# Scores of a local attention by query halves as 64x64 tiles of TensorE, a block-diagonal product as 128x32 tiles, and some reordering in the first half

## What is computed

```python
h = layernorm(x) * (1 + ca) + sa
x = x + ga * attn(h)        # 3 layers: causal linear attention, 16 heads, FFN of 1024
h = layernorm(x) * (1 + cb) + sb
x = x + gb * ffn(h)         # 2 layers: local attention, 8 heads of 64, gated FFN of 682
...
def causal_linear_attention(q, k, v):      # first half, per token
    S += k v^T ; z += k
    out = (q S) / (q z + 1e-6)
...
def local_attention(q, k, v):              # second half, windows of 128 tokens
    # queries of window w see keys of windows w-1 and w
    mask = (i < j) | (i > j + 128) | (j == -1)
    attn = softmax(where(mask, -max, (8 q) k^T))
    out = attn v
```

## Time and profile before

| | |
|---|---|
| median of 3 runs | 2609.28 us (2607.87 to 2610.86) |
| the profiled execution, its own time | 2610.22 us |
| its span | 2608.4 us |
| PE busy | 2523.3 us, 97% |
| DVE busy | 2143.9 us, 82% |
| ACT busy | 1405.0 us, 54% |
| POOL busy | 1427.1 us, 55% |
| mean granted TensorE clock | 0.989 of full |

### The profile page before, as it was taken

How to read it: one execution, slowest core, us unless ns; L and a number is a source line. 1 busy time by engine, 2 the same in 40 slices (tenths; PEclk the granted TensorE clock), 3 DMA queues, 4 the chain that set the end, 5 groups by cost and what they waited for, 6 DMA issues and landing times.

```text
span 2608.4 us, 65564 instructions
## 1 busy us (share of the span) xinstructions
PE 2523.3 (97%) x23520; PEld 2094.4 (80%) x23520; DVE 2143.9 (82%) x5253; ACT 1405.0 (54%) x2945; POOL 1427.1 (55%) x1406
## 2 busy tenths in 40 slices
PE   6899999999999999999998999999999999999998
PEld 4688888888888888887776788888888888888877
DVE  5798888887787788898999887888898887888875
ACT  3343344334433443344256777777776777777761
POOL 2253444443444355455576666666676766776664
PEclk8899999999999999999999999999999999999999
DMA  3100000010000010000112000000111100110001
GB/s 91 38 18 10 18 2 18 14 36 2 2 2 14 14 42 10 18 26 26 49 38 66 21 17 19 12 16 17 32 32 36 33 29 23 32 32 28 27 29 49
DMA packets 79088, 67.44 MB, mean 26 GB/s; under 512 B 15896, under 2 KB 73368, under 8 KB 78776
## 3 DMA queue, kind: packets, MB, share of 16 engines
q1 hardware_dynamic: 78776, 63.25, 8.1%
HBM read 49.18 MB, written 12.58 MB: 24 GB/s over the span
## 4 chain that ended last, share of the span: by engine, by line
PE 87%; DVE 6%; issue 3%; ACT 2%; POOL 1%; DMA 0%; SPq 0%; DVEq 0%; ACTq 0%; POOLq 0%
PE PS L276 76%; PE PS L974 4%; PE PS L936 1%; PE PS L1004 1%; PE PS L927 1%; PE PS L488 1%; PE PS L498 1%; PE PS L431 1%; PE PS L885 1%; DVE U L3159 1%; DVE PS L3567 1%; PE PS L1034 1%; DVE Z L2997 0%; ACT PR L2227 0%; DVE X L3005 0%
## 5 line engine op out<-in xcount | busy, mean ns | idle before, releaser
L2227 ACT ACTIVATE PR<-PS,SM 128x256 f32<-128x256 f32 (+1 forms) x512 | 280.7, 561 | 136.5 <-DVE SM L3572 135.9
L1913 ACT ACTIVATE FB<-PS,BC 128x512 f32<-128x512 f32 x192 | 133.5, 695 | 322.1 <-PE PS L276 174.9
L3159 DVE TENSOR_TENSOR U<-PS,CST 128x512 f32<-128x512 f32 x384 | 238.0, 681 | 37.5 <-PE PS L276 37.4
L4597 POOL TENSOR_TENSOR RL<-FB,RH 128x512 fp32r<-128x512 f32 x96 | 125.7, 1310 | 219.6 <-DVE RH L3136 219.6
L4819 POOL TENSOR_TENSOR SM<-SM,COL 128x8 f32<-128x8 f32 x128 | 224.6, 1755 | 10.7
L276 PE MATMUL PS<-W2H,RH 128*128 128x256 f32 x768 | 226.1, 294 | 2.2 <-POOL RL L4597 2.2
L3567 DVE CUSTOM_DVE_ANT_0 PS<-PS,MSK 128x256 f32<-128x256 f32 (+1 forms) x512 | 202.5, 436 | 30.5 <-PE PS L276 29.5
L276 PE MATMUL PS<-W2H,RL 128*128 128x256 f32 x768 | 215.8, 281 | 0.0
L276 PE MATMUL PS<-W2L,RH 128*128 128x256 f32 x768 | 215.7, 281 | 0.0
L4609 POOL TENSOR_TENSOR SBD<-SBD,TMP 128x256 f32<-128x256 f32 x84 | 64.8, 772 | 197.0 <-DVE TMP L3151 197.0
L276 PEld LDWEIGHTS PS<-W2H,RH 128*128 128x128 f32 x768 | 145.0, 189 | 25.0 <-issue 20.4
(11 more groups left out here) (268 smaller groups left out, 8467.4 us busy)
## 6 DMA issues: line engine op xcount, KB each, us to landing
PX<-in_L_attn_x SPq DMA_DIRECT2D x16, 512.0 KB, 3.9
TB<-in_k_rot SPq DMA_DIRECT2D x64, 128.0 KB, 2.1
SG<-in_L_attn_W SPq DMA_DIRECT2D x24, 256.0 KB, 2.8
xp_scratch<-PX SPq DMA_DIRECT2D x8, 512.0 KB, 2.9
xs_scratch<-X SPq DMA_DIRECT2D x64, 64.0 KB, 1.5
ZS<-xs_scratch SPq DMA_DIRECT2D x16, 256.0 KB, 2.8
GG<-xp_scratch SPq DMA_DIRECT2D x7, 512.0 KB, 3.7
out<-GG SPq DMA_DIRECT2D x7, 512.0 KB, 2.9
```

Of the source, the lines that this page charges most:

```text
L1913: e.activation(FB[:, hb % 2, :], PS[:, 5, :], ACT.Relu, bias=BC[:, l % 2, 4 + hb:5 + hb]).then_inc(*a_re.up(n, hb))
L2227: t = e.activation(PR[:, par, 256 * i + lo:256 * i + hi], PS[:, 3 + par, 256 * i + lo:256 * i + hi], ACT.Exp, bias=S[:, 40 + 2 * g + i:41 ...
L3159: e.tensor_tensor(heads(U[:, u % 6, :], 4), heads(PS[:, g, :], 4), bcast(CM, 4), ALU.mult).then_inc(*d_mk.up(n, u))
L4597: e.tensor_tensor(RL[:, r, :], FB[:, 0, :], RH[:, r, :].bitcast(F), ALU.subtract).then_inc(*p_rl.up(n, hb))
```

## The change

1. `scores_tile` splits the 128 queries in two halves of 64. A matmul now has 64 rows and 64 columns (par picks the rows, half the columns and the output partitions), and multiplies 192 keys instead of 256: for the lower half the whole window before and the lower 64 keys of its own, for the upper half the upper 64 keys of the window before and its whole own window. The region left out is the one that the mask covers.
2. The keys are stored with the two buffers beside each other for each pair of heads (`keys_of`), so that for odd tiles the 192 keys are one run of columns, and one matmul. For even tiles the window before lies behind the own window, and each half has two matmuls, of 128 and 64 keys or 64 and 128. Columns of scores, PR and PT now always have the window before first, so `blocks`, the masks and the copies lose their cases.
3. In `sums` the product with SBD is made of four matmuls of 32 columns instead of one of 128.
4. DVE: for chunks 1, 2 and 23 both `add_bv` steps stand ahead of `gate_steps(1)` and `modulate_b(2)`, of `modulate_a(3)`, and of `norm2_b(20)`.
5. PE, end of the first half: `up(22, 1)` stands ahead of `down(21, 6)` and `up(22, 5)` ahead of `ask_v(0)`.

```diff
+    def keys_of(b):
+        return KT.rearrange("p x (h b n) -> p (x h) b n", h=2, b=2)[:, :, b, :]
...
                 for m in range(2):
-                    mm(e, PS[:, 4, 128 * m:128 * m + 128], SBD[:, tile % 2, m, :], FQ[:, m, 0, 128 * j:128 * j + 128], m == 0)
+                    for g in range(4):
+                        mm(e, PS[32 * g:32 * g + 32, 4, 128 * m:128 * m + 128], SBD[:, tile % 2, m, 32 * g:32 * g + 32], FQ[:, m, 0, 128 * j:128 * j + 128], m == 0)
...
             for i in range(2):
+                c = 128 * (2 * hf + i)
                 for par in range(2):
-                    r, c = slice(64 * par, 64 * par + 64), slice(128 * (2 * hf + i), 128 * (2 * hf + i) + 128)
-                    if first:
-                        m = mm(e, PS[:, 3 + par, 256 * i + 128 * cur:256 * i + 128 * cur + 128], QT[r, c], KT[r, cur, c], i == 0)
-                    else:
-                        m = mm(e, PS[:, 3 + par, 256 * i:256 * i + 256].rearrange("p (b n) -> p b n", b=2), QT[r, c], KT[r, :, c], i == 0)
+                    for half in range(2):
+                        r, p, a = slice(64 * par, 64 * par + 64), slice(64 * half, 64 * half + 64), 256 * i
+                        Q = QT[r, c + 64 * half:c + 64 * half + 64]
+                        if first or cur == 0:
+                            before, here = 128 if half == 0 else 64, 64 if half == 0 else 128
+                            if not first:
+                                mm(e, PS[p, 3 + par, a + 128 - before:a + 128], Q, keys_of(1 - cur)[r, 2 * hf + i, 128 - before:128], i == 0)
+                            m = mm(e, PS[p, 3 + par, a + 128:a + 128 + here], Q, keys_of(cur)[r, 2 * hf + i, 0:here], i == 0 and first)
+                        else:
+                            m = mm(e, PS[p, 3 + par, a + 64 * half:a + 64 * half + 192], Q, KT[r, hf, 256 * i + 64 * half:256 * i + 64 * half + 192], i == 0)
...
-            return (u % 2,) if u % 16 == 0 else (0, 1)
+            return (1,) if u % 16 == 0 else (0, 1)
...
-                e.copy(KT[:, u % 2, :], PS[:, 7, :]).then_inc(*b_kt.up(u))
+                e.copy(keys_of(u % 2), PS[:, 7, :].rearrange("p (h n) -> p h n", h=4)).then_inc(*b_kt.up(u))
...
         gate_steps(0)
+        add_bv(1, 0)
+        add_bv(1, 1)
         gate_steps(1)
-        add_bv(1, 0)
         modulate_b(2)
-        add_bv(1, 1)
...
         splits(23, "a")
         norm3_b(19)
-        norm2_b(20)
         splits(23, "v")
         add_bv(23, 0)
         add_bv(23, 1)
+        norm2_b(20)
```

More of the change, by code:

```diff
@@ L992, in mix @@
                         start = hf == 0 and i == 0 and b == blocks(u)[0]
-                        v = u if b == u % 2 else u - 1
+                        v = u - 1 + b
                         m = mm(e, PS[64 * par:64 * par + 64, 2, 128 * hp:128 * hp + 128], VV[:, v % 3, 64 * (2 * hp + par):64 * (2 * hp + par) + 64],
@@ L1174, in _ @@
         down(21, 5)
+        up(22, 1)
         down(21, 6)
-        up(22, 1)
         up(22, 2)
@@ L1189, in _ @@
         down(22, 2)
+        up(22, 5)
         ask_v(0)
-        up(22, 5)
         up(22, 6)
@@ L2218, in exps @@
             hf, par, S = g // 2, g % 2, SM[:, u % 4, :]
-            lo, hi = (128 * (u % 2), 128 * (u % 2) + 128) if u % 16 == 0 else (0, 256)
+            lo, hi = 128 if u % 16 == 0 else 0, 256
             e.wait_ge(*g_bi[g].at(u))
@@ L3290, in _ @@
         add_bv(2, 0)
+        add_bv(2, 1)
         modulate_a(3)
-        add_bv(2, 1)
         split(10)
@@ L3559, in largest @@
             hf, par, S = g // 2, g % 2, SM[:, u % 4, :]
-            lo, hi = (128 * (u % 2), 128 * (u % 2) + 128) if u % 16 == 0 else (0, 256)
-            z = 128 if u % 16 == 0 else (0 if u % 2 else 128)
+            lo, hi = 128 if u % 16 == 0 else 0, 256
             if u == 0:
@@ L3566, in largest @@
                 o = PS[:, 3 + par, 256 * i + lo:256 * i + hi]
-                t = e.tensor_tensor_reduce(o, o, MSK[:, z:z + hi - lo], 1.0, NEG, ALU.add, ALU.max, S[:, 32 + 2 * g + i:33 + 2 * g + i])
+                t = e.tensor_tensor_reduce(o, o, MSK[:, lo:hi], 1.0, NEG, ALU.add, ALU.max, S[:, 32 + 2 * g + i:33 + 2 * g + i])
             t.then_inc(*g_tt[g].up(u))
```

## The result

The changed kernel takes 2587.11 us (median of 4 runs, 2584.52 to 2589.78) against 2608.66 us (2607.87 to 2610.86) for the kernel before, in the same session. The ratio is 0.9916, with a 95% interval of 0.9899 to 0.9933: faster by 21.9 us, give or take 4.4. The forecast was 2578, its range 2566 to 2594. So direction and range held, but the gain of 31.4 us that the sum promised is 43% larger than the measured one, and the time lies just outside the likeliest case's own range of 2570 to 2586. The stated range held because it had been drawn out to the faster rivals. The profiled execution took 2584.52 us around a span of 2582.7, 25.7 less than the one before.

The account below looks back on a forecast made before the run. The prediction took TensorE (PE) to bound most of the kernel, DVE the first tiles of the second half. Its terms, 22.3 + 2 + 3.4 + 3.2 + 0.5 = 31.4 us, gave 2578 us, range 2566 to 2594.

Parts of the forecast that it names:

- likeliest case's own range: Whole kernel: 2570 to 2586 us if the main forecast, given a chance of 0.68, holds.
- faster rivals: Even tiles held back, 2594 us, chance 0.10; waits taking half the scores' gain, 2589 us, chance 0.12.
- Scores in tiles 8 to 61: PE-bound stretch: 54 odd steps save 0.25 us each, 49 even ones 0.23; 24.8 us, of which 22.3 kept.
- the risk (passes for one quarter in a row): Even scores tiles: quarters starting late would make a step 1.16 us instead of 0.83; as a rival 2594 us, chance 0.10.
- The allowance of a tenth: PE-bound stretch: a tenth of the scores' 24.8 us gain turns into waits, 2.5 us either way.
- the prediction's sign: Later tiles: a group of four gets 1.9 us shorter; PE idle growing by more than 5 us would mean waits.
- rival of waits: PE-bound stretch: half the scores' gain returns as waits for exponentials and output rows; 2589 us, chance 0.12.
- Tiles 0 to 7 and the last: Tiles 0 to 3 gain nothing, DVE-bound; 11 steps in tiles 4 to 7, 62 and 63 save 2.6 us, 2 kept.
- Chunk 23: Earlier biases remove the 3.00 us wait before favor, plus 0.4 us for the clock; 3.4 us, bounds 2 and 4.7.
- Chunks 1 and 2: Earlier biases shorten the waits before favor: 3.2 us at chunk 1, bounds 1.5 and 5, and 0.5 at chunk 2.
- SBD and the order of pieces: Split SBD product and reordered up and down pieces: no gain, bounds 2 us and 1 us each way.
- Slower rival: Scores: column halves don't overlap when rows are split too; odd step 1.45 us, even 1.50; 2649 us, chance 0.05.

Follow-up runs that it names:

- even_grouped: Changed kernel with the even tiles' short scores passes reordered, for both query halves 128 columns first, then 64; ratio 0.9913 to the kernel before.
- turn_later: Changed kernel with turn_tile one step later, behind the step that followed it, in 21 places; ratio 0.9948 to the kernel before.
- turn_some: Changed kernel with turn_tile moved behind ask_q only where ask_q followed it, in 12 tiles; ratio 0.9903 to the kernel before.
- scores_only: Kernel before with the new scores step alone, its masks and the keys' new places; ratio 0.9941 to the kernel before.
- bias_only: Kernel before with only the biases of chunks 1, 2 and 23 moved earlier; ratio 0.9982 to the kernel before.
- order_only: Kernel before with only the two moves of up and down pieces on PE; ratio 1.0003 to the kernel before.
- sbd_only: Kernel before with only the summed keys' product (SBD) split into 128x32 tiles; ratio 1.0004 to the kernel before.

## Why the forecast was right in sign and too large

Sorted by the prediction's own terms:

- Scores in tiles 8 to 61: 22.3 forecast, 12.8 in the trace. This is the mis-sized term. The odd step came out as forecast, 0.811 against 0.81. The even step is 0.895 instead of 0.83, which costs 3.1 us; the prediction saw the risk (passes for one quarter in a row) but priced all or nothing, and it was a partial one, shown by even_grouped. The allowance of a tenth, 2.5 us, for lost cover was the step that failed: 4.6 us were lost ahead of `turn_tile`, 1.8 behind it, 1.0 behind `turn_weights`, about 0.5 in a few single long scores steps, and 1.1 in pieces of 0.24 us or less by kind, whose cause is open. The prediction had even named "the output product that waits for `mixed`", but not `turn_tile`, which waits for it too; I read PE's idle time, 0.3 us, as slack, when `OO` ended 0.26 us before the step that overwrites its bank and 0.15 is the least. turn_later and turn_some show this wait. A group of four tiles became 0.95 us shorter on average, where the prediction's sign was 1.9; PE's idle time grew by 3.8 us, under the 5 that it had set as the sign of waits, since most of the waits don't show there.
- Its rival of waits (2589) was nearer in time than the forecast, and half right in its mechanism. Of 24.8 us, 12.8 arrived, half as it said, and the largest wait is one for output rows, `OO`. But 3.1 of the loss is the size of the even step, and the waits are mostly not for exponentials, as it also had in mind: one bank is handed over in too short a time. That the time still fell within the range is owed to this rival's place in it.
- Tiles 0 to 7 and the last: 2 forecast, sc0-sc8 is 4.0 shorter in the trace and 1.7 in scores_only, which has the same program there. So the two executions of one program differ by 2.4 us, and the term is not tested.
- Chunk 23: 3.4 forecast, 3.1 in every trace with the edit. Right.
- Chunks 1 and 2: 3.7 forecast, 4.3 in this pair of traces, yet that can be chance. The step that failed is "`modulate_b(2)` (3.57 us) and `gate_steps(1)` leave the path": 3.57 is what it takes beside POOL, 1.66 is what it takes alone, and in that case the wait is 2.24 us in the old order too. f0-f2 is 96.09 to 101.09 us in the four traces with the old order and 94.26 to 100.06 in the ten with the new one, so the edit is worth something between 0 and 3 us there, by an estimate from these. bias_only bought 4.7 us, of which chunk 23 explains 3.1.
- SBD and the order of pieces: nothing forecast, nothing measured. f23-sc0 is 2.4 us shorter in this pair of traces but 0.4 in order_only, and kernels with the changed program there lie between 76.04 and 78.71, so that is no gain of this change.
- Slower rival: rows and columns split together do overlap. In the odd steps the first passes on the four tiles start 7 ns apart. The rule of strict order (the Trainium skill, TensorE: Matmul & The Clock Gate, part 3), which the prediction weighed, would not allow this if the two passes of each matmul stand one behind the other; the trace disagrees with it for 64x64 tiles too. Even steps disagree for whole matmuls: their first four passes start within 40 ns and last 320, 267, 320 and 267 ns, which are passes of 128, 64, 128 and 64 columns. In program order 128 and 64 columns for the first tile come ahead of 64 for the second, so the third matmul started before the second.
- The profiled execution of before lay at the slow end of its own spread (101.09 us from f0 to f2, where the others have 94 to 100), so the traces differ by 25.7 us and the medians by 21.6.

## What to carry to other kernels

When a step on the bounding engine gets shorter, list what stands right behind it and, for each, by how much its other operand was already there; a margin smaller than the saving becomes the new bound, and the list of waits need not show it, so compare starts. Two gains that end at the same hand-over don't add up, as the 14 even steps of even_grouped show. Price a stall from more than one execution, and look whether another engine stretches the instruction that causes it.

## What the hardware showed that I had not expected

- Four scalings of 128x256 on DVE take 3.57 us beside two POOL subtractions and 1.66 us without them; which of the two it is changes between executions of the same code (before and order_only run the same code there).
- 32 passes on four 64x64 tiles take 0.895 us when the quarters receive 128 and 64 columns out of step, 0.829 when in step. The number of instructions is the same.
- 64x64 tiles cost nearly the same as 64x128 ones: an odd step of 256 columns takes 1.03 us on four tiles and 1.06 on two, an even step, cut into 128 and 128 columns, 1.10.
- Matmuls on different tiles start out of program order: in an even step the third, known by its length, starts 14 ns after the first, while the second has the first one's tile to wait for.
- A wait of 2.67 us of PE was followed by a mean granted clock of 0.68 over 5.4 us; behind one of 1.05 us it stayed at 1.00, but behind one of 3.19 us at the same place in sbd_only too.
